# Expert phase of a Mamba and mixture-of-experts block: token search on PE, experts in pairs, scatter-adds two at a time

## What is computed

```
logits = x @ gate_w;  w, idx = top_k(softmax(logits), 8);  w = w / sum(w)
pos    = how many earlier (token, choice) pairs chose the same expert
buf[e, pos] = x[token]              for pos < 128
gu     = buf @ expert_gate_up_w;    act = silu(gu[:, :128]) * gu[:, 128:]
out_e  = act @ expert_down_w
y[token] += w * out_e[e, pos];      result = x + y + shared
```

## Time and profile before

| | |
|---|---|
| runs | 4618.23, 4619.41, 4621.55 us |
| profiled execution, first to last instruction | 4617.3 us |
| device time of the profiled execution | not recorded apart from its span |
| GpSimd (POOL) busy | 88% |
| VectorE (DVE) / TensorE (PE) / ScalarE (ACT) busy | 83% / 79% / 71% |
| main phase | 0 to about 4200 us |
| what is left of the last sequence | 4200 to 4273 us |
| search and experts | 4273 to 4617.3 us |

### The profile page before, as it was taken

The page is one execution under the profiler, slowest core; times in us unless marked ns, Lnnn a source line. Parts: engine busy times, 40 slices in busy tenths (PEclk is TensorE's granted clock), DMA queues, the critical chain, the costliest instruction groups (busy, mean ns, idle before and its releaser), DMA issues.

```text
span 4617.3 us, 56113 instructions
## 1 busy us (share of the span) xinstructions
PE 3632.1 (79%) x16000; PEld 2285.9 (50%) x16000; DVE 3829.4 (83%) x3990; ACT 3280.2 (71%) x4895; POOL 4074.0 (88%) x2223
## 2 busy tenths in 40 slices
PE   3588888888888888888888888888888888876465
PEld 1354555555545555555555545554555454553344
DVE  2899989898989988889989999888989899882433
ACT  3687778787777877878777777787877778772111
POOL 3999999999999999999999999999999999991576
PEclk7798999899999989999989999999989999988666
DMA  3222222222222222222222222222222221220665
GB/s 121 87 75 74 79 80 99 95 99 99 94 100 75 72 66 94 96 98 100 99 95 99 75 72 72 88 99 95 99 99 94 100 75 71 74 77 17 173 158 131
DMA packets 147381, 423.30 MB, mean 92 GB/s; under 512 B 15520, under 2 KB 98656, under 8 KB 113776
## 3 DMA queue, kind: packets, MB, share of 16 engines
q1 hardware_dynamic: 123504, 362.73, 21.3%
q0 software_dynamic: 23552, 56.64, 6.5%
HBM read 333.17 MB, written 52.59 MB: 84 GB/s over the span
## 4 chain that ended last, share of the span: by engine, by line
POOL 39%; issue 22%; DVE 19%; PE 9%; ACT 8%; DMA 2%; POOLq 0%; DVEq 0%; ACTq 0%; SPq 0%
POOL hs L377 19%; POOL hs L386 13%; DVE ps L1165 9%; ACT ps L537 3%; DVE hs L1165 3%; PE ps L884 2%; DVE hs L1175 2%; PE ps L814 2%; DVE xc L1069 2%; POOL dtu L433 2%; PE ps L858 1%; POOL hs L473 1%; POOL rstd L399 1%; DVE xn L1090 1%; ACT L537 1%
## 5 line engine op out<-in xcount | busy, mean ns | idle before, releaser
L377 POOL TENSOR_TENSOR hs<-dtu,b_all 128x1024 f32<-128x1024 f32 x1024 | 2409.4, 2373 | 3.4
L537 ACT ACTIVATE ps<-dt,neg_a 128x512 f32<-128x512 f32 x2048 | 1327.2, 682 | 290.0 <-DVE hs L1175 146.5
L814 PEld LDWEIGHTS ps<-ident,hs 128*128 128x128 f32 x8192 | 1013.9, 151 | 584.9 <-issue 393.3
L1165 DVE TENSOR_TENSOR_SCAN ps<-ps,hs 128x1024 f32<-128x1024 f32 x544 | 1244.2, 2287 | 46.0 <-ACT ps L537 23.8
L814 PE MATMUL ps<-ident,hs 128*128 128x128 f32 x8192 | 1151.4, 290 | 117.3 <-POOL hs L386 75.8
L1165 DVE TENSOR_TENSOR_SCAN hs<-ps,hs 128x1024 f32<-128x1024 f32 x480 | 1088.1, 2278 | 170.2 <-ACT ps L537 147.4
L386 POOL TENSOR_TENSOR hs<-hs,c_all 128x1024 f32<-128x1024 f32 x480 | 1137.0, 2369 | 59.5 <-DVE hs L1165 46.1
L1175 DVE TENSOR_TENSOR hs<-ps,c_all 128x1024 f32<-128x1024 f32 x544 | 665.7, 1224 | 34.4
L924 PE MATMUL ps<-mT,w_sgu 128*128 128x512 f32 x1024 | 522.4, 635 | 12.5 <-DVE hid L1122 9.0
L858 PE MATMUL ps<-xd,w_dt 32*128 32x512 f32 x256 | 185.3, 810 | 234.0 <-ACT dt L609 223.1
L537 ACT ACT_TABLE_LOAD x219 | 281.0, 1283 | 117.3 <-POOL dt L435 113.9
(11 more groups left out here) (127 smaller groups left out, 4448.9 us busy)
## 6 DMA issues: line engine op xcount, KB each, us to landing
b_all<-bc SPq DMA_DIRECT2D x128, 1024.0 KB, 6.0
c_all<-bc SPq DMA_DIRECT2D x128, 1024.0 KB, 7.9
dt<-dtu POOLq DMA_DIRECT2D x64, 512.0 KB, 4.6
table<-rows SPq DMA_DIRECT2D x32, 640.0 KB, 3.8
xin<-x SPq DMA_DIRECT2D x32, 512.0 KB, 3.5
out<-mT SPq DMA_DIRECT2D x32, 512.0 KB, 3.7
c_all<-egu_w SPq DMA_DIRECT2D x64, 256.0 KB, 2.8
c_all<-edown_w SPq DMA_DIRECT2D x64, 128.0 KB, 3.0
```

The costliest lines, as they stand in the source:

```text
L377: pool.tensor_tensor(ring(h, hf, n), dtu[:, JH * hf:JH * hf + JH, :], b_all[:, n, :].unsqueeze(1).broadcast_to([P, JH, L]), ALU.mult)\
L537: i = act.activation(state_of(n)[:, k, :], dt[:, j, :], ACT.Exp, scale=neg_a[:, j, n:n + 1])
L814: m = pe.matmul(ybank[:, i, k * P:(k + 1) * P], ring(h, hf, n)[:, k, i * P:(i + 1) * P], ident[:, :], start=False, stop=(n == N - 1), is_t ...
L1165: dve.tensor_tensor_scan(inputs if s in ON_POOL else whole, whole, inputs, 0.0, ALU.mult, ALU.add).then_inc(state_ready, 1)
```

## The change

In the main phase `count` becomes four matmuls of 128 columns, each tile of 128 tokens counted for itself, and `read_counts` one plain copy to bf16: no totals are carried and no tile ends are made. `counts` becomes an array of 128 tiles x 64 experts x 128 tokens in bf16.

After the last turn the counts are loaded to SBUF with a tile in each partition, 124 tiles early and the last four when they are there. One matmul with a triangle of ones sums the tiles' totals. ScalarE makes two shifted copies of each expert's counts (`shift_counts`, 2 x 127 elements), VectorE two bf16 matrices of ones and zeros for each group of four experts (`sets`, EG = 4), and PE multiplies them (`pick_rows`, eight bf16 matmuls for each group), which puts the counts of slot c's tile in partition c; `tokens` compares and sums them for four experts at once. The gathers of tile counts are gone. Three groups (FOUND) are done before the first expert, the others between experts.

Experts are taken in pairs. For each slot of the pair's second expert `match` finds whether its token is also in the first expert's slots; a matmul (`join`) moves such rows' results over, VectorE adds them to the first expert's result (`add_joint`), and the second expert's copies of them are sent to rows past the output. A pair has then no row twice, and its two scatter-adds run together; the next pair waits for both. GpSimd's order is, for pair u: gathers of experts 2u+4 and 2u+5, the wait for `e_res` of pair u, the wait for all earlier scatter-adds, the two scatter-adds. PE's order in its step e is gate_up(e), transposes of e+1, down(e-1), and at odd e join((e-3)/2). ScalarE scales the results (`weigh`) in VectorE's place. Rows and weights have rings of eight, each expert's weights come in one DMA (laid out on the host), and everything after the main phase is unrolled.

```diff
--- before
+++ after
...
+        tile_counts = b_all[:, 0:E * P // (2 * L), :].rearrange("p n l -> p (n l)").bitcast(BF16)
         got = pieces(0, ER, ROW)
...
+                act.copy(cnt[:, :], pobank[0:E, :]).then_inc(post_read, 1)
...
                 for i in range(NT):
...
+                    m = pe.matmul(pobank[0:E, i * P:(i + 1) * P], maskb[:, i, :], steps_tri[:, :], start=True, stop=True)
...
+            tiles = counts.rearrange("t e k -> t (e k)")
+            known = TILES - NT
+            sp.wait_ge(counts_stored, 16 * (B - 1))
+            sp.wait_ge(input_ready, B * NS)
+            sp.dma_start(tile_counts[0:known, :], tiles[0:known, :]).then_inc(early_in, 16)
+            sp.wait_ge(readout_ready, vector_reads(B, 0))
+            sp.wait_ge(pool_readout, pool_reads(B, 0))
+            def weights(e, r):
+                wait(sp, e_o, e - ER + 1)
+                sp.dma_start(flat[:, r * 768:(r + 1) * 768], expert_w[e]).then_inc(e_weights[r], 16)
+            for e in range(ER):
+                weights(e, e)
             store_rows(B - 1)
...
-
+            store_counts(B - 1)
+            sp.wait_ge(counts_stored, 16 * B)
+            sp.dma_start(tile_counts[known:TILES, :], tiles[known:TILES, :]).then_inc(late_in, 16)
             sp.wait_ge(consts, CONSTS + 1)
             sp.dma_start(out[T:T + CAP, :], xd[:, 0:DM]).then_inc(pad_stored, 16)
...
             store_out(B - 1)
...
+            for e in range(ER, E):
+                weights(e, e % ER)
...
+            def gather(e):
+                pool.wait_ge(in_ready, e // EG + 1)
+                wait(pool, e_res, e // 2 - ER // 2 + 1)
+                pool.indirect_dma_start(out=got[e % ER], out_offset=None, in_=table,
+                                        in_offset=bass.IndirectOffsetOnAxis(ap=row_in[:, e:e + 1], axis=0))\
+                    .then_inc(e_gathered[e % ER], 16)
+            def scatter(e):
+                pool.indirect_dma_start(out=out, out_offset=bass.IndirectOffsetOnAxis(ap=row_out[:, e:e + 1], axis=0),
+                                        in_=res_e[e % ER], in_offset=None, compute_op=ALU.add).then_inc(e_scattered, 16)
...
             for e in range(AHEAD):
-                gather(e, e)
-
+                gather(e)
             pool.wait_ge(out_stored, 16 * B)
             pool.wait_ge(pad_stored, 16)
...
+            for u in range(E // 2):
+                for e in (2 * u, 2 * u + 1):
+                    if e + AHEAD < E:
+                        gather(e + AHEAD)
+                pool.wait_ge(out_ready, 2 * u // EG + 1)
+                pool.wait_ge(e_res, u + 1)
+                wait(pool, e_scattered, 32 * u)
+                for e in (2 * u, 2 * u + 1):
+                    scatter(e)
...
+            def shift_counts(e):
+                g, i = e // EG, e % EG
...
+                if i == 0:
+                    wait(act, rows_picked, g - 1)
+                one = tile_counts[:, e * P:e * P + P - 1]
+                act.activation(plus[g % 2][:, i, 0:P - 1], one, ACT.Identity, bias=starts[:, e:e + 1])
+                act.activation(minus[g % 2][:, i, 0:P - 1], one, ACT.Identity, bias=back[:, e:e + 1], scale=-1.0)\
+                    .then_inc(shifted, 1)
...
+            def weigh(e):
+                act.wait_ge(e_o, e + 1)
+                wait(act, e_scattered, 32 * (e // 2 - ER // 2 + 1))
+                act.activation(res_e[e % ER], ps[:, 4 + e % 2, 0:DM], ACT.Identity,
+                               scale=got[e % ER][:, DM + e:DM + e + 1]).then_inc(e_scaled, 1)
+            for e in range(FOUND * EG):
+                shift_counts(e)
             copy_rows(0, 0)
...
+            for e in range(E + 1):
+                if e < E:
+                    gate(e)
                 if e + 1 < E:
                     copy_rows(e + 1, e + 1)
+                if e > 0:
+                    weigh(e - 1)
+                if e + FOUND * EG < E:
+                    shift_counts(e + FOUND * EG)
...
+            def add_counts():
+                pe.wait_ge(early_in, 16)
+                pe.wait_ge(late_in, 16)
+                pe.wait_ge(post_read, B * POST_USES)
+                pe.matmul(pobank[:, 0:E], steps_tri[:, :], tile_counts[:, P - 1:E * P:P], start=True, stop=True)\
+                    .then_inc(summed_up, 1)
+            def pick_rows(g):
+                pe.wait_ge(shifted, EG * g + EG)
+                pe.wait_ge(sets_ready, g + 1)
+                wait(pe, picked_read, g)
+                for i in range(EG):
+                    pe.matmul(ps[:, 6, i * P:(i + 1) * P], from_start[g % 2][:, i, :], plus[g % 2][:, i, :],
+                              start=True, stop=False)
+                    m = pe.matmul(ps[:, 6, i * P:(i + 1) * P], from_stop[g % 2][:, i, :], minus[g % 2][:, i, :],
+                                  start=False, stop=True)
+                m.then_inc(rows_picked, 1)
+            def turn_rel(g):
+                pe.wait_ge(rel_ready, g + 1)
+                wait(pe, same_ready, g)
+                for k in range(EG // 2):
+                    e = EG * g + 2 * k
+                    m = pe.transpose(ps[:, 1, k * P:(k + 1) * P], rel[:, e:e + 1].broadcast_to([P, P]), ident[:, :])
+                m.then_inc(rel_turned, 1)
...
+            def join(u):
+                pe.wait_ge(e_scaled, 2 * u + 2)
+                pe.wait_ge(same_ready, 2 * u // EG + 1)
+                wait(pe, e_res, u)
+                pe.matmul(pobank[:, DM:2 * DM], same[2 * u // EG % 4][:, u % (EG // 2), :], res_e[(2 * u + 1) % ER],
+                          start=True, stop=True).then_inc(e_joint, 1)
+            add_counts()
+            pick_rows(0)
+            for g in range(FOUND):
+                if g + 1 < FOUND:
+                    pick_rows(g + 1)
+                turn_rel(g)
             turn_rows(0, 0, 0)
...
+            for e in range(E + 3):
+                if e < E:
+                    gate_up(e)
+                if e + 1 < E:
+                    turn_rows(e + 1, 0, 0)
+                if 0 < e <= E:
+                    down(e - 1)
+                if e % 2 == 1 and e >= 3:
+                    join((e - 3) // 2)
+                g = e // EG + FOUND
+                if g < E // EG and e % EG == EG - 1:
+                    pick_rows(g)
+                if FOUND < g <= E // EG and e % EG == 1:
+                    turn_rel(g - 1)
...
+            def sets(g):
+                es = slice(EG * g, EG * g + EG)
+                wait(dve, rows_picked, g - 1)
+                across = slots[:, :].unsqueeze(1).broadcast_to([P, EG, P])
+                dve.tensor_tensor(from_start[g % 2], across, starts[:, es].unsqueeze(2).broadcast_to([P, EG, P]),
+                                  ALU.is_ge)
+                dve.tensor_tensor(from_stop[g % 2], across, stops[:, es].unsqueeze(2).broadcast_to([P, EG, P]),
+                                  ALU.is_ge).then_inc(sets_ready, 1)
+            def tokens(g):
+                es = slice(EG * g, EG * g + EG)
+                row = ps[:, 6, :].rearrange("p (k m) -> p k m", k=EG)
+                dve.wait_ge(rows_picked, g + 1)
+                dve.tensor_scalar(fits[g % 2][:, :, 0:P - 1], row[:, :, 0:P - 1], slot[:, 0:1], None, ALU.is_le)\
                     .then_inc(find_step, 1)
...
+                dve.wait_ge(find_step, 3 * g + 1)
+                dve.tensor_reduce(before[:, es], fits[g % 2][:, :, 0:P - 1], AX.X, ALU.add).then_inc(find_step, 1)
+                dve.wait_ge(find_step, 3 * g + 2)
+                dve.tensor_tensor(before[:, es], before[:, es], row[:, :, P - 1], ALU.add).then_inc(picked_read, 1)
+                dve.wait_ge(picked_read, g + 1)
+                dve.tensor_scalar(rel[:, es], before[:, es], slot[:, 0:1], None, ALU.min).then_inc(find_step, 1)
+                dve.tensor_scalar(row_in[:, es], before[:, es], float(T), float(T - 1), ALU.add, ALU.min)\
+                    .then_inc(in_ready, 1)
+                dve.wait_ge(find_step, 3 * g + 3)
+                dve.tensor_scalar(row_out[:, EG * g:EG * g + EG:2], rel[:, EG * g:EG * g + EG:2], float(T), None, ALU.add)\
+                    .then_inc(rel_ready, 1)
+            def match(g):
+                odd = slice(EG * g + 1, EG * g + EG, 2)
+                dve.wait_ge(rel_turned, g + 1)
+                wait(dve, e_joint, EG // 2 * (g - 3))
+                dve.tensor_tensor(same[g % 4], ps[:, 1, 0:EG // 2 * P].rearrange("p (k m) -> p k m", k=EG // 2),
+                                  rel[:, odd].unsqueeze(2).broadcast_to([P, EG // 2, P]), ALU.is_equal)\
+                    .then_inc(same_ready, 1)
+                dve.wait_ge(same_ready, g + 1)
+                dve.tensor_reduce(twice[:, odd], same[g % 4], AX.X, ALU.add).then_inc(same_step, 1)
+                dve.wait_ge(same_step, 2 * g + 1)
+                dve.scalar_tensor_tensor(rel_b[:, odd], twice[:, odd], 2.0 * T, rel[:, odd], ALU.mult, ALU.add)\
+                    .then_inc(same_step, 1)
```

(29 more changed lines are left out.)

## The result

The median of 12 runs is 4632.35 us (4620.62 to 4636.78), against 4619.68 us before (12 runs): a ratio of 1.0026, 95% interval 1.0018 to 1.0034. The kernel became slower by a quarter of a percent. The forecast was 4613 us, 0.14% faster: the sign was wrong, the time inside the range.

What follows compares the result with a forecast made beforehand. POOL's own DMAs and the serial scatter-adds were taken to bound the expert phase. Search, ramp, loop and tail +2 us, main phase -8: -6 against the 4617.3 span, 4611.3; time 4613 us, range 4580 to 4650.

Steps and rivals of the forecast that it cites:

- the loop through one pair with its five members: Expert phase: PE work, add_joint, handoff to POOL, two scatter issues, gather to transposes; 9.9 to 10.0 us a pair.
- the gather at 3.3 us: Loop term: from the gather's start to PE's transposes 3.3 us, with weight loads overlapping half of the gathers.
- the search: Between last count and first transposes: PE's first rows only after three early groups, near 4295; gains some 2 us.
- the ramp: From the first transposes to the first scatter-add, with join(0) in PE's step 3: about 14 us.
- the tail: Last two pairs have no gather and wait only for landings: 20.4 us to the end.
- two landings at 6.6: A pair's two scatter-adds, the second 1.92 us behind the first, land after 6.7 us in the forecast.
- VectorE to POOL: Loop term: handoff from VectorE's end to POOL's scatter-add, 0.3 us from one row of the kernel before.
- Together 2.4 or 1.33: Loop term: PE's transposes, down and join, 2.4 us at low clock, 1.33 at full; 2.0 taken at granted clock 0.67.
- that stretch by `sets`: Expert phase: VectorE's tensor_tensors beside POOL's scatter issues cost nothing; if they blocked, 8 us in all.
- took 8 and called 10 the bound: Main phase: ScalarE's shorter copy saves 0.3 us a turn, at most 10 us, at least nothing; 8 taken.
- the fast loop of 9.0: Rival for the expert loop: PE mostly at full clock, gathers clear of weight loads; 29 us less, 4584; chance 0.22.
- the one with the gather behind two scatter-adds: Rival for the expert loop: gather queues behind two scatter-adds, up to 12.9 us a pair, 4697; half, 4654; chance 0.24.

Runs made afterwards that it cites:

- e4: Changed kernel with seven unused float32 matmuls of 256 columns on PE ahead of the transposes that wait for the gather; 4612.86 us, ratio 0.9983.
- e6: Changed kernel with ScalarE's old work per turn put back (copy with bias, wait, small copy of tile ends), PE's count staying short; ratio 1.0084, 4654.79 us.
- e9: Kernel before with ScalarE's read_counts cut to a plain copy, PE's long count kept, scatter-adds sent past the output; 4608.44 us, ratio 0.9967.
- e12: e9 with PE's count also cut to four matmuls of 128 columns; 4618.84 us, ratio 0.9989 to the kernel before.
- e8: e1 with weights loaded for the first eight experts only, the other 56 reusing them (another result); 4508.70 us, ratio 0.9765.
- e1: Changed kernel with AHEAD raised from 4 to 6, so gathers run six experts ahead; 4539.21 us, ratio 0.9828.
- e2: Changed kernel with the gathers for experts 2u+6 and 2u+7 issued ahead of pair u's two scatter-adds instead of behind them; 4542.26 us, ratio 0.9825.
- e10: Changed kernel with gathers six ahead and, on PE, down and join ahead of the transposes; 4531.34 us, ratio 0.9796.
- e11: Changed kernel with two memsets of 128 x 2048 on POOL behind each pair's gathers; 4631.04 us, ratio 1.0018.
- e5: Changed kernel with POOL waiting for the earlier scatter-adds first and the pair's result last; 4634.14 us, ratio 1.0025.

## Why the prediction was wrong

**What held.** The bounds in the kernel before; POOL's relief; the loop through one pair with its five members in their order; the gather at 3.3 us (3.33 from its start to the transposes, mean of 29); the search (24.5 us, 23.7 forecast, and PE's first rows only after all three groups); the ramp (first transposes to first scatter-add 13.8 us, 14 forecast); the tail (20.2 us from 4609.03, 20.4 forecast); two landings at 6.6. Of the marks set for the changed kernel all came, but for the period, 10.81 us, just above the 9.5 to 10.5 named, and the end of the last turn, some 14 us earlier instead of 8.

**The steps that failed** are two terms of the round, and one of the main phase. The round, term by term:

| term | forecast, us | mean of 29 rounds, us |
|---|---|---|
| two scatter-adds, to the gather's start | 3.8 | 3.90 |
| gather's start to the transposes | 3.3 | 3.33 |
| transposes, down and join, to `add_joint` | 2.0 | 2.28 |
| `add_joint` | 0.5 | 0.42 |
| VectorE's end to the scatter-add's start | 0.3 | 0.88 |
| sum | 9.9, taken as 10.0 | 10.81 |

- "VectorE to POOL: 4302.88 to 4303.16 = 0.3." It was 0.87 in nearly every pair: 0.58 x 29 = 17 us. I took one row, the first scatter-add; three of the next four in the same trace had 0.5, and the chain of the tail before, which I had read too, showed 0.8 to 0.9 from the end of POOL's wait for a landing to the next scatter-add. A member of a loop needs its price from several rows.
- "Together 2.4 or 1.33; at 0.67, that is two thirds of the time at the low level, 2.0." The mean clock of the phase was even higher (0.77), yet this part took 2.4 us in 19 of the 29 rounds and 1.4 in only three: it comes right behind a wait of 4 to 5 us for the gather, and the clock behind such a wait was mostly the low one. 0.28 x 29 = 8 us; e4 shows it from the other side. A mean over the phase does not hold for the work that stands behind the idle time.
- Beyond these, the first scatter-add of every second pair took 1.82 us instead of 1.62, in 12 pairs, 2.4 us in all, and `add_joint` was a little shorter. The prediction had left that stretch by `sets` at nothing. The round came out at 10.8 for 10.0: +23.5 us.
- The main phase gave 14.0 us where I took 8 and called 10 the bound. The bound was wrong: ScalarE's shorter work alone is worth 22 to 24 us by e6 and e9. It counted the copy's time and left out what its end does at the loop's edge. The 14.0 is itself uncertain, for two of nine executions of the same main phase lie only 8 to 9 us below the kernel before. Whether PE's shorter count is free stays open: e9 and e12 speak for a cost of about 10 us, but don't settle it.

So the forecast's -6 us had to be -6 + 23.5 - 6 = +12 us, and this is what was measured. The mechanism was right and the sizes of these terms were off, and since the forecast lay so near to no change, they decided the sign. That the time fell inside the range owes something to luck: its upper end allowed 11.2 us a pair, for a stretched scatter issue and the low clock; the handoff, the largest error, was not among its reasons.

Of the rivals, the fast loop of 9.0 was never there (the shortest of the 29 rounds was 9.96); the one with the gather behind two scatter-adds had the sign and the wrong place: the gather kept its 3.3 us, and in e8, where a gather also follows two scatter-adds, it lands after 2.9. The Trainium skill's page "DMA: Bandwidth & Descriptors", section "Two DMAs through the same engine are not ordered", lets descriptors of one queue start in order and overlap. This trace agrees: at 4609.03 us two scatter-adds were issued 1.92 us apart, and the second had landed 5.7 us behind the first one's start, where one alone takes 3.8 from issue to landing.

The other page of the Trainium skill that the prediction names, "SBUF — State Buffer", section "Who interferes with whom", infers that a tensor_tensor with two SBUF inputs takes only the read side of the shared ports, which descriptors don't need; it also says that such an instruction contends with a GpSimd instruction that reads SBUF. Here it did hold POOL up a little. In the changed kernel, a scatter-add's issue took 1.82 us instead of 1.62 when one of the tensor_tensors of `sets` was running as it began, and 1.61 again in the last pairs, without `sets`. It moves with `sets`: in e1, e2 and e8 it is some second scatter-adds (1.8 to 2.1 us instead of 1.58) and some gathers (up to 1.46 instead of 1.02) that are stretched, each with a tensor_tensor of `sets` running at its start. None of the more than 100 issues in each of these traces without `sets` beside them was as long, nor was one beside which `sets` began later. Not every issue that began under `sets` was stretched, and what exactly waits isn't shown.

The expected gain of taking away 64 tile gathers and half of the waits for landings went into the loop: the landing of two scatter-adds would have allowed 6.6 us a pair, and 10.8 were needed. e1 and e10 show that most of it was there to be had (7.6 and 7.2 us).

## What to carry to other kernels

When the stages behind a prefetch are deepened, lay the program orders of the issuing and the consuming engine side by side and count again how many items lie between the result that releases a prefetch and the item that it fetches; here one constant (four to six) was worth 2%. Price each handoff inside a loop from several rows, and what runs right behind a wait at the clock that it finds there. An operation at the end of a hardware loop's body can cost more than its duration. And before a difference of one mark between two profiles is read as a cause, look how far the same mark moves between kernels that do the same up to it; here it was 17 us.

## What the runs showed of the hardware

- Matmuls that are never read made the kernel faster, 4612.9 against 4632.4 us: granted clock 0.91 instead of 0.79 (4290 to 4500 us), and 1.68 us instead of 2.28 in the mean for the same three steps (e4).
- 384 KB of weight loads per expert moved the median landing of a scatter-add from 3.8 to 4.5 us and of a gather from 2.9 to 4.0 (e8, e1, over 4300 to 4520 us).
- An indirect DMA whose issue began while a tensor_tensor with two SBUF inputs ran on VectorE was mostly stretched, a scatter-add from 1.6 to 1.8 up to 2.1 us, a gather from 1.0 to as much as 1.46; one beside which the tensor_tensor began later was not (changed kernel, e1, e2, e8).
- In the changed kernel POOL started an indirect DMA 0.30 us behind the one before it, but 0.87 us behind the VectorE instruction that it waited for. It was the same after 4.5 us of idle time and after 1.45 (e11), and 0.90 with the waits in the other order (e5). The kernel before had 0.3 to 0.5 at its first such places; the reason isn't known.
- With an extra wait and a small copy as the last work of a hardware loop's body, ScalarE's next instruction started 3.5 us behind the count copy, without them 0.5 (before and e6 against the changed kernel).
- Nine kernels with the same main phase ended it between 4246.9 and 4264.0 us, one profiled execution of each.
